# The router's first matrix folded into the cells' matrix, and a new order of work in a mixture-of-experts stage

## The reference, cut to what matters

```
spikes_enc = sigmoid(inputs_embeds @ enc_W + enc_b)             # 128 -> 256
cont = flat @ s2c_W + s2c_b                                     # 256 -> 64, the "cells"
logits = tanh(cont @ rW1 + rb1) @ rW2 + rb2                     # the router, 64 -> 64 -> 8
probs = softmax(logits); topw, topi = top_k(probs, K)
w = topw / topw.sum(-1, keepdims=True)
gates = (one_hot(topi, E) * w[..., None]).sum(1)
h = relu(einsum('nm,emh->enh', cont, We1) + be1)                # 64 -> 128 per expert
expert_out = einsum('enh,ehm->enm', h, We2) + be2
output_flat = einsum('enm,ne->nm', expert_out, gates)
spikes_moe = sigmoid(output_flat @ c2s_W + c2s_b)               # 64 -> 256
decoded = sigmoid(spikes_moe @ dec_W + dec_b)                   # 256 -> 128
return layernorm(decoded, ln_g, ln_b)
```

## Time and profile before

| | |
|---|---|
| median of three runs | 1439.51 us |
| profiled execution | 1435.92 us |
| its span in the profile | 1433.8 us |
| mean granted TensorE clock in it | 0.945 of full |
| TensorE busy with matmuls | 1203.1 us, 84% |
| VectorE, ScalarE, GpSimd busy | 913.2 (64%), 904.9 (63%), 638.9 (45%) |
| the experts' stage | from 1022.7 to the end |
| TensorE busy between 1022 and 1434 | 351.21 of 412.00 us |
| first matmul of `cells` in rounds 2, 4, 6, 12, 15 | 1076.28, 1118.67, 1162.15, 1301.09, 1365.66 |
| GpSimd's gain multiplication in round 6 | from 1167.74 |

### The profile page before, as it was taken

One profiled execution on the slowest core, in us unless ns is written; L12 is line 12 of the kernel. 1 busy time (PEld: TensorE's weight loads), 2 busy tenths in 40 slices (PEclk: granted clock), 3 DMA queues, 4 the chain that ended last, 5 costly groups with the idle time before them and its releaser, 6 DMA issues. The chain is left out here.

```text
span 1433.8 us, 27085 instructions
## 1 busy us (share of the span) xinstructions
PE 1203.1 (84%) x7434; PEld 529.8 (37%) x7434; DVE 913.2 (64%) x2874; ACT 904.9 (63%) x1342; POOL 638.9 (45%) x1047
## 2 busy tenths in 40 slices
PE   4698999999999999948996092999589999999983
PEld 1122222222222222214664092677324333333431
DVE  4477777777777777755996857334355675666542
ACT  2588999999999999933554360333335656566553
POOL 5344556565656664233555300000233555555444
PEclk9999999999999999978999596999889999999997
DMA  4665556555555545149200030000000000000000
GB/s 123 125 118 91 106 103 112 111 104 104 110 107 106 107 100 100 26 95 251 81 0 1 30 118 1 0 0 0 0 1 1 8 16 7 15 15 8 16 16 22
DMA packets 71177, 87.95 MB, mean 61 GB/s; under 512 B 10136, under 2 KB 64958, under 8 KB 65214
## 3 DMA queue, kind: packets, MB, share of 16 engines
q1 hardware_dynamic: 69078, 85.55, 28.6%
q10 hardware_dynamic: 2024, 1.51, 0.5%
HBM read 63.84 MB, written 31.59 MB: 67 GB/s over the span
## 5 line engine op out<-in xcount | busy, mean ns | idle before, releaser
L493 ACT ACTIVATE a_probs<-a_S 128x1024 f32<-128x1024 f32 x512 | 496.6, 1035 | 74.7 <-DVE a_S L635 67.2
L635 DVE TENSOR_TENSOR a_S<-a_S,a_tables 128x256 f32<-128x256 f32 (+1 forms) x512 | 281.3, 561 | 157.5 <-PE a_S L509 154.6
L516 PE MATMUL a_O<-a_probs,a_V 128*32 128x512 f32 x2048 | 275.0, 609 | 2.4 <-ACT a_probs L493 0.6
L509 PE MATMUL a_S<-a_Qs,a_Ks 48*128 48x512 bf16 x1024 | 180.0, 389 | 27.5 <-DMA a_Qs<-a_parts_dram 14.7
L509 PEld LDWEIGHTS a_S<-a_Qs,a_Ks 48*128 48x128 bf16 x1024 | 42.7, 93 | 243.0 <-ACT a_probs L493 194.6
L2005 ACT ACTIVATE e_hid<-e_H 128x512 f32<-128x512 f32 x128 | 69.5, 594 | 80.1 <-PE e_H L2110 80.1
L413 POOL CAST a_parts<-a_whole 128x512 bf16<-128x512 f32 x47 | 29.1, 620 | 157.9 <-DVE a_whole L645 148.8
L1758 ACT ACTIVATE g_hid<-g_H,w_b 128x512 f32<-128x512 f32 x64 | 44.0, 688 | 86.9 <-PE g_H L1779 86.9
L1917 POOL MEMSET e_rT<- 1x512 f32 x1 | 0.5, 518 | 215.8 <-POOLq L1733 215.8
L2108 PE MATMUL e_H<-e_gated,w_We 64*128 64x512 f32 x256 | 74.6, 659 | 12.4 <-DVE e_gated L2208 10.4
L2119 PE MATMUL e_O<-e_hid,w_We 128*64 128x512 f32 x256 | 73.7, 627 | 0.5 <-ACT e_hid L2005 0.5
(11 more groups left out here) (344 smaller groups left out, 2313.7 us busy)
## 6 DMA issues: line engine op xcount, KB each, us to landing
a_parts_dram<-a_parts SPq DMA_DIRECT2D x94, 192.0 KB, 5.6
a_Qs<-a_parts_dram SPq DMA_DIRECT2D x64, 192.0 KB
a_Qs<-a_parts_dram SPq DMA_DIRECT2D x64, 128.0 KB
m_taps_by_step<-h_taps SPq DMA_DIRECT2D x8, 1024.0 KB, 13.5
m_taps<-m_taps_by_step SPq DMA_DIRECT2D x8, 1024.0 KB, 5.2
a_Ks<-a_parts_dram SPq DMA_DIRECT2D x30, 192.0 KB
XY<-L_attn_x SPq DMA_DIRECT2D x16, 256.0 KB, 7.2
a_Qs<-a_parts_dram SPq DMA_DIRECT2D x64, 64.0 KB
```

The source lines that it names most:

```text
L493: act.activation(probs[n % KEPT][:], S[n % RING][:], ACT.Exp).then_inc(exped, 1)
L509: mm = pe.matmul(S[n % RING][:, par, :], Ks[p][rows, pr, kb * P:(kb + 1) * P], Qs[p][Q_OF(kb)][rows, pr, :], start=True, stop=True)
L516: mm = pe.matmul(O[VC * j:VC * (j + 1), :], V[q][:, kb, HG * g + j, :], probs[(2 * m + j // 2) % KEPT][:, j % 2, :], start=(kb == 0), stop ...
L635: v.tensor_tensor(s[:, :, where], s[:, :, where], wide, ALU.mult).then_inc(corrected, 1)
```

## The change

The product of the cells' matrix and the router's first matrix is computed once, at the start of the stage: two transposes of `s2cW` on TensorE, a copy on VectorE, two matmuls and one for the bias, an addition and a copy on VectorE. In a round, `cells` then puts the router's sums (weights `s2rW`) into partitions 0 to 63 and the cells (weights `s2cW`) into 64 to 127. The router's matmul goes. ScalarE takes the tanh from the cells' bank. VectorE adds the bias with two instructions from the one half, for each of the two halves that the experts read.

The order of a round changes too. On TensorE the logits stand ahead of spread 0, the decoding is cut into two halves around `expert_in` 0, and each of spreads 1 to 3 stands ahead of the `expert_in` before which it stood behind. On VectorE the logits are taken ahead of `weigh` 0, and each part of `choose` ahead of the next `weigh`; the moments of `shaped` stand behind `weigh` 2 and no longer ahead of `weigh` 1. On ScalarE the tanh is first, and the normalisation of `decoded` moves from the end of a round to behind the tanh of the next. On GpSimd the inversion for `shaped` stands behind the layer norm.

```diff
@@ experts
+        s2rW, s2cT, s2rb = sb("s2rW", [P, HC, M]), sb("s2cT", [M, HC * P]), sb("s2rb", [64, 1])
+        router, cells_rows = slice(0, 64), slice(M, 2 * M)
...
-        dec_use, logits_use, next_xT_use = (lambda i, k=k: i * 3 + k for k in (2, 3, 4))
+        logits_use, dec_use, next_xT_use = (lambda i, k=k: i * 3 + k for k in (2, 3, 4))
...
@@ GpSimd, body
-                if shapes:
-                    shaped.invert(pool, i - 3, shaped.rstd)
-                    shaped.offset(pool, i - 3)
...
                     if not isinstance(i, int) or i < B - 2:
                         layer_norm(i + 2)
+                if shapes:
+                    shaped.invert(pool, i - 3, shaped.rstd)
+                    shaped.offset(pool, i - 3)
@@ ScalarE, body
+                if a:
+                    FB.read(act, cont_use(i))
+                    act.activation(rT[0:64], FB.t[router], ACT.Tanh, bias=s2rb[:]).then_inc(heard, 1)
+                if shapes:
+                    decoded.wait(act, i - 3)
+                    normalise(i - 3, decoded.rstd, decoded.offsets, normed[1])
                 if c:
                     cells_to_spikes(c2s_use(i))
-                if a:
-                    FB.read(act, router_use(i))
-                    FB.emptied(act.activation(rT[0:64], FB.t[0:64], ACT.Tanh, bias=W.rb1[:]))
...
-                if c:
-                    decoded.wait(act, i - 2)
-                    normalise(i - 2, decoded.rstd, decoded.offsets, normed[1])
@@ TensorE
+            for m in range(HC):
+                mm = pe.transpose(FB.t[0:M, tile_of(core, m)], W.s2cW[:, m, :], core.ident[:])
+            mm.then_inc(folded, 1)
...
-                    for h in range(2):
-                        mm = pe.matmul(FB.t[h * M:(h + 1) * M], W.s2cW[:, m, :], enc[:, m, :], start=(m == 0),
+                    for to, w in ((router, s2rW), (cells_rows, W.s2cW)):
+                        mm = pe.matmul(FB.t[to], w[:, m, :], enc[:, m, :], start=(m == 0),
...
-                FB.filled(pe.matmul(FB.t[0:64], W.rW1[:], contT[p][0:M], start=True, stop=True))
...
+            pe.wait_ge(folded, TAKEN)
+            for m in range(HC):
+                pe.matmul(FB.t[:, m * M:(m + 1) * M], s2cT[:, tile_of(core, m)], W.rW1[:], start=True, stop=True)
+            pe.matmul(FB.t[0:64, HC * M:HC * M + 1], W.rW1[:], W.s2cb[0:M], start=True, stop=True).then_inc(folded, 1)
             encoder(FIRST_XT, 1)
+            pe.wait_ge(folded, MERGED)
@@ VectorE
-                FB.emptied(v.tensor_scalar(contT[p][:], FB.t[:], W.s2cb[:], None, ALU.add))
+                v.tensor_scalar(contT[p][cells_rows], FB.t[cells_rows], W.s2cb[cells_rows], None, ALU.add)
+                FB.emptied(v.tensor_scalar(contT[p][0:M], FB.t[cells_rows], W.s2cb[cells_rows], None, ALU.add))
...
+            v.wait_ge(*W.experts)
+            v.wait_ge(folded, TURNED)
+            v.tensor_copy(s2cT[:], FB.t[0:M, 0:HC * P]).then_inc(folded, 1)
             prepare = Tally(v, joined.steps)
...
+            v.wait_ge(folded, FOLDED)
+            v.tensor_tensor(s2rb[:], FB.t[0:64, HC * M:HC * M + 1], W.rb1[:], ALU.add)
+            v.tensor_copy(s2rW[:].rearrange("p m k -> p (m k)"), FB.t[:, 0:HC * M]).then_inc(folded, 1)
```

More of the change, by code:

```diff
@@ L1872, in experts @@
         gap_done, share_done, gates_done = sem("gap_done"), sem("share_done"), sem("gates_done")
+        folded, heard = sem("folded"), sem("heard")
+        TURNED, TAKEN, FOLDED, MERGED = range(1, 5)
         FIRST_XT = 1
-        dec_use, logits_use, next_xT_use = (lambda i, k=k: i * 3 + k for k in (2, 3, 4))
-        decoded_use = lambda i, more: dec_use(i) if more else dec_use(i) - 2
+        logits_use, dec_use, next_xT_use = (lambda i, k=k: i * 3 + k for k in (2, 3, 4))
+        decoded_use = lambda i, a, b: i * 3 + (3 if a else 2 if b else 0)
         next_enc_use = lambda i: i + 2
-        cont_use, router_use = (lambda i: i * 2 + 1), (lambda i: i * 2 + 2)
+        cont_use = lambda i: i + 1
         gatesT_use = lambda i: i * 5 - 4
@@ L2128, in spikes, with decode @@
                     HB[m].filled(pe.matmul(HB[m].t[:], W.c2sW[:, tile_of(core, m)], moeT[:], start=True, stop=True))
[L2130 to L2136, removed]
+            def decode(i, n, half):
+                if half == 0:
+                    for m in range(HC):
+                        HB[m].after(pe, c2s_use(i))
+                    TP.fill(pe, n)
+                    pe.matmul(TP.t[:], W.ones16[:], W.decb[:].rearrange("p c d -> p (c d)"), start=True, stop=False,
+                              skip_group_check=True)
+                for c in range(half * NT // 2, (half + 1) * NT // 2):
                     for m in range(HC):
@@ L2139, in decode @@
                                        start=False, stop=(m == HC - 1), skip_group_check=True)
-                TP.filled(mm)
+                if half:
+                    TP.filled(mm)
             def body(i, p, a, b, c, more, **_):
@@ L2152, in body @@
                 if a:
-                    FB.after(pe, cont_use(i))
-                    router(i, p)
+                    logits(i)
                 if b:
@@ L2158, in body @@
                 if c:
-                    decode(i, decoded_use(i, a or b))
-                elif b or a:
+                    decode(i, decoded_use(i, a, b), 0)
+                elif a:
+                    TP.after(pe, logits_use(i))
                     skip(TP, dec_use(i))
                 if b:
+                    spread_gates(i, 1)
                     expert_in(i, 0)
-                    spread_gates(i, 1)
-                if a:
-                    logits(i)
+                if c:
+                    decode(i, decoded_use(i, a, b), 1)
                 if b:
+                    spread_gates(i, 2)
                     expert_in(i, 1)
-                    spread_gates(i, 2)
                     expert_out(i, 0)
@@ L2245, in body @@
                     take_gates(i)
+                if a:
+                    tick.begin(i)
+                    take_logits(i)
+                if b:
                     weigh(i, 0, 1 - p)
-                if shapes:
-                    v.wait_ge(summed[1], (i - 3) * 2 + 2)
-                    shaped.moments_of(v, i - 3, Y[:, i - 2])
+                if a:
+                    TP.after(v, logits_use(i))
+                    choose(0)
                 if isinstance(i, int) and i == 0:
@@ L2255, in body @@
                 if a:
-                    tick.begin(i)
-                    take_logits(i)
-                    TP.after(v, logits_use(i))
-                    choose(0)
+                    choose(1)
                 if b:
                     weigh(i, 2, 1 - p)
-                if a:
-                    choose(1)
+                if shapes:
+                    v.wait_ge(summed[1], (i - 3) * 2 + 2)
+                    shaped.moments_of(v, i - 3, Y[:, i - 2])
                 if b:
@@ L2268, in body @@
                 if c:
-                    TP.after(v, decoded_use(i, a or b))
+                    TP.after(v, decoded_use(i, a, b))
                     decoded.moments_of(v, i - 2, Y[:, i - 1])
```

11 lines of the change are left out of this document (4 added, 7 removed).

## The result

The changed kernel takes 1446.43 us (median of five runs, 1445.79 to 1449.64), the one before 1439.51 (1437.04 to 1440.86). The ratio is 1.0058, with a 95% interval of 1.0041 to 1.0074: slower by 0.58%, 6.9 us, where 1.5 was forecast (1441). The profiled execution took 1446.43, its span is 1444.2.

A forecast was written before the change was run, and what follows sets the result against it. TensorE bound packed rounds; loop rounds also waited on GpSimd's bias through VectorE and lost clock. Terms +2.1, -4.2, -0.1, +3.2, start and tail 0 made +1.0, onto the median 1439.51: 1440.5, rounded 1441 us (1433 to 1453).

The forecast's parts named there:

- The bound step: ScalarE's sigmoid waits for the second decoding half, relus queue behind it; `expert_in` 1 starts 11.1 after `cells`, 1.07 later.
- Rounds 2 and 3: Two packed rounds ahead of the loop, each 1.07 us longer by the later `expert_in` 1: +2.1 us.
- round 12: The round at 22.2 us against 22.32 before: -0.1 us.
- rounds 13 to 15: Last rounds outside the loop, lengthened by the later `expert_in` 1: +3.2 us.
- The loop: Eight rounds; stalls on GpSimd's bias and slow clock go, 1.07 a round added: 178.2 against 182.42, -4.2 us.
- the clock rival: TensorE's new 1.65 us stall drops the clock in half of 14 rounds: 7 x 1.5 = +10.5, 1451 us; 22%.
- The start and rounds 0 and 1: Stage's start +1.3, round 0 -1.9, round 1 +0.6 us: together 0.
- The matrix copy: Stage's start: VectorE's first step waits for two transposes and a 64x256 copy, 0.9 + 0.4 = +1.3 us (0.5 to 2.5).
- transposes-to-`cells` piece: Stage's start: folded matmuls fall into the wait for xnT and the encoder's time; nothing, 0.8 us if not.
- VectorE beside GpSimd: Steps of `choose(0)` lengthened beside GpSimd, weigh 1 ends 10.2 to 10.5; one operation more delays `expert_in` 1: 1455 us; 9%.
- The main forecast: Expected case: weigh 1 ends at 8.4, relus set `expert_in` 1, 1441 us (1438 to 1446); 50%.
- Packed at 20.13: TensorE packed if relus were not held behind the sigmoid: rounds of 20.13, -28 us in all, 1411; 6%.

The follow-up runs named there:

- run 1: Changed kernel with ScalarE's relus of experts 0 and 1 ahead of the decoded bank's sigmoid: 1428.93 us, 0.9925 of the kernel before.
- run 5: Changed kernel with the decoding undivided again, all of it ahead of `expert_in` 0, ScalarE's order left: 1431.03 us, 0.9951 of the kernel before.
- run 9: Changed kernel with round 0's moments of sequence 2 between the logits' copy and `choose(0)`: a single execution of 1444.11 us, no ratio.
- run 7: Changed kernel with VectorE's copy of the transposed cells' matrix behind the moments of the first two sequences: ratio 1.0049 to the kernel before.
- run 2: Changed kernel with VectorE's `weigh` 1 ahead of `choose(0)` and `weigh` 2 ahead of `choose(1)`: 1447.39 us, 1.0054 of the kernel before.
- run 3: Changed kernel with both the relus ahead of the decoded bank's sigmoid and weighings 1 and 2 ahead of the choices: 1429.70 us, 0.9925 of the kernel before.
- run 8: Changed kernel with round 0's moments of sequence 2 ahead of the logits' copy and `choose(0)`: 1445.87 us, 1.0048 of the kernel before.
- run 4: Kernel before, all its orders kept, with only the folded matrix and two-output `cells` added: 1440.83 us, 1.0012 of the kernel before.
- run 6: Changed kernel with the decoding undivided and weighings 1 and 2 ahead of the choices, ScalarE's order left: 1440.10 us, 1.0016 of the kernel before.
- run 11: Changed kernel, all corrections together, round 0's moments behind the logits' copy, experts' sum copied ahead of `joined`'s moments: 1428.81 us, 0.9932 of the kernel before.
- run 12: The 1428.81 us version of all corrections, with ScalarE's normalisation of `decoded` moved behind the spikes' sigmoids: 1419.01 us, 0.9879 of the kernel before.

## Why the prediction was right, and where it was not

The direction and the step that sets the time came as forecast. The time came less well: 1446.43 lies inside the stated range of 1433 to 1453, but just above the forecast's own 1438 to 1446. That it is so near is partly luck. From one profiled execution to the other the sum had +1.0 and 10.4 was measured; the times differ by only 6.9 because the profiled execution of before was 3.6 under its median. Of the 9.4 that the sum missed, 4.3 lie in the start with rounds 0 and 1, 3.8 in the loop, and 1.4 ahead of the stage, in code that both kernels share.

- *The bound step was right.* "ScalarE's queue still has the sigmoid of the decoded bank AHEAD of the relus": 11.15 measured for 11.1, and run 1 takes that part of the loss away by moving one instruction; run 5 does so by filling the bank earlier. Rounds 2 and 3 cost +1.99 (2.1 forecast), round 12 -0.20 (-0.1), rounds 13 to 15 +3.0 (3.2).
- *The loop* was forecast at -4.2 and came to -0.45. The six rounds at full clock are 22.3 to 22.4, 0.1 over the forecast; the rest is two rounds of 24.0 where the clock fell. This is the clock rival in a small dose: "it decides from two slow rounds on", and two there were. In the first of them the clock fell right behind the stall, although dense decoding stood ahead of it, which the prediction held against this rival: spread 2 had waited 1.36, and `expert_in` 1 behind it took 1.94 instead of 1.13. It isn't the same in every execution: run 9 leaves the loop as it is and has none (178.73 at 1.00), run 7 has one (180.43). I gave the rival 22 points as a case of seven rounds or none; the two in between belonged into the forecast as a term of about +3.

```profile
1137.13 0.39 PE L2103 MATMUL e_G<-e_gatesT,w_select 128*128 128x512 bf16 x1 [1.36 <-DVE e_gated L2219]
1137.65 1.94 PE L2111 MATMUL e_H<-e_gated,w_We 64*128 64x512 f32 x4
```

- *The start and rounds 0 and 1* were the term mis-sized: 0 forecast, +4.30 measured. The matrix copy cost 2.26, not 1.3 (inside the bounds of 0.5 and 2.5): I allowed 0.9 until it could start, but TensorE's transposes start only 1.27 into the stage and the copy at 2.00 (1026.09, with the stage at 1024.09). The transposes-to-`cells` piece cost 0.35, put at nothing. Round 0 gave back 2.53 (1.9 forecast) with its `cells` at full clock, as before; in runs 1, 2, 3 and 5, with the lower level, the same instructions gave back only 0.6. Round 1 cost 4.22, far over the bound of 1.0: I counted VectorE's few operations there as if they ran alone, and left out both GpSimd's beside them and the clock. At `expert_in` 0 1.3 were lost (it starts 8.15 after `cells`, 6.83 before), with TensorE standing 2.35 ahead of spread 0; the other 2.9 came behind it, where the matmuls ran at the lower level until about 1073.0 and `expert_in` took 2.08 instead of 1.13. Runs 8 and 9 show that moving the moments of sequence 2 alone doesn't bring it back. Why the clock stayed down for so long was not tested.
- *VectorE beside GpSimd*: the rival's mechanism is there as priced (two steps lengthened), its end at 10.04 in round 13 and 10.09 to 10.75 in the loop, for the 10.2 to 10.5 worked out, still ahead of ScalarE (in the loop's first round by some 0.2). The main forecast had put it at 8.4, so its condition, that the wait would be for the relu alone, did not hold. It cost nothing here, and 0.7 to 0.9 in most rounds as soon as ScalarE's order was mended (run 1).
- *Packed at 20.13* was out of reach. The best versions have 20.54: the decoding's first matmul came about 0.2 later (5.76 for 5.55) than in the round before the change, and TensorE waits 0.25 for the relus ahead of the fourth `expert_in`, where a spread had stood.
- *Where 16 x 1.00 us of TensorE's work went*: before, the matmul had filled a wait for the gates (run 4). After, the logits fill that wait, and the microsecond is lost again, with one more, in front of `expert_in` 1.

## What to carry to other kernels

An instruction on the bound engine is worth what the engine would wait without it: look at what arrives last behind it before you count its length as a gain. When a reader's input is made later (here by cutting its producer in two), look at what is queued behind that reader on its engine, not only at the reader. Several waits of nearly one length may stand behind each other: each experiment that takes one away tells only of the next, so a single edit without effect does not show that it was free.

## What the runs showed of the hardware

- Two sets of weights in the two column halves run side by side like one set twice: pairs start 0.01 to 0.04 apart, and the next matmul, `spikes`, starts 1.85 after `cells` as it did before (1332.27 - 1330.42).
- A VectorE step of 0.17 to 0.19 that reads two arrays takes 0.8 to 1.3 where it starts early beside a GpSimd operation of 512 columns (1.04 to 1.27 us), and a reduction of one array does not. Beside GpSimd's L184 (four columns, 1.02 us) a step with two arrays takes 0.19. The weighing, which reads one array from SBUF and one from PSUM, stays at 0.69. One input is no safe sign either: a cast of 96 columns, 0.21 alone, took 0.98 in run 8 (1058.89). Which steps are hit depends on a microsecond's shift, so an edit of VectorE's order moves the damage rather than removes it (runs 6, 8 and 9).
- The clock's price per round: 24.0 for 22.3 in the changed kernel (+1.7), 23.2 for 21.1 in run 11 (+2.1); the number of such rounds went from none to three between executions and orders, and none of the loop's rounds of 20.6 to 21.1 in run 12 had the lower clock.
